# A graph network's edge loop with a ring of 16 gathered groups, node units in three steps, and a prologue in five parts

## The reference

```python
h = jnp.maximum(_layernorm(x, axis=-1), 0.0)
...
h = x @ enc_w + enc_b
h_list = [h]
for l in range(n_layers):
    e = edge_attr @ edge_w[l] + edge_b[l]
    msg = jax.nn.relu(h_list[l][src] + e)
    agg = jax.ops.segment_sum(msg, dst, num_segments=n_nodes)
    z = (1.0 + eps[l]) * h_list[l] + agg
    z = jax.nn.relu(z @ mlp_w1[l] + mlp_b1[l]) @ mlp_w2[l] + mlp_b2[l]
    h_list.append(jax.nn.relu(z))
hcat = jnp.concatenate(h_list, axis=1)
return hcat @ out_w + out_b        # and x is added
```

## Time and profile before

| | us |
|---|---|
| median of 3 timed runs | 6492.11 (6486.08 to 6496.12) |
| span of the profiled execution | 8994.4 |
| first gather starts, in the profiled execution | 111.24 |
| last gather starts, in the profiled execution | 8945.59 |
| POOL busy | 4756.1 |
| PE busy | 5354.3 |
| DVE busy | 1804.5 |
| ACT busy | 1006.8 |

### The profile page before, as it was taken

The page is one execution under the profiler, slowest core; times in us unless marked ns, Lnnn a source line. Parts: engine busy times, 40 slices in busy tenths (PEclk is TensorE's granted clock), DMA queues, the critical chain, the costliest instruction groups (busy, mean ns, idle before and its releaser), DMA issues.

```text
span 8994.4 us, 89832 instructions
## 1 busy us (share of the span) xinstructions
PE 5354.3 (60%) x21970; PEld 4659.5 (52%) x21971; DVE 1804.5 (20%) x4266; ACT 1006.8 (11%) x1630; POOL 4756.1 (53%) x5030
## 2 busy tenths in 40 slices
PE   5565656556565566555665556565556555655556
PEld 4555555555555455555555555554555555555555
DVE  5111111111111111111111111111111111111112
ACT  3111111111111111111111111111111111111111
POOL 4555555555555455555555555545555555555554
PEclk7555555555555555555555555555555555555555
DMA  4111111111111111111111111111111111111112
GB/s 134 44 44 45 44 44 45 44 44 44 43 43 44 41 46 45 45 45 44 44 44 43 45 44 44 45 41 45 44 43 46 44 45 43 44 43 45 44 44 66
DMA packets 342770, 422.04 MB, mean 47 GB/s; under 512 B 183228, under 2 KB 249840, under 8 KB 342624
## 3 DMA queue, kind: packets, MB, share of 16 engines
q0 software_dynamic: 159456, 326.88, 14.2%
q1 hardware_dynamic: 144327, 75.77, 3.3%
q10 hardware_dynamic: 38976, 19.27, 0.7%
HBM read 388.55 MB, written 41.09 MB: 48 GB/s over the span
## 4 chain that ended last, share of the span: by engine, by line
PE 36%; another core or an unknown queue 35%; issue 16%; DVE 5%; DVEq 5%; ACT 2%; ACTq 0%; DMA 0%; POOL 0%; POOLq 0%; SPq 0%
PE bank L562 17%; PE bank L555 14%; DVEq L767 2%; PE bank L587 2%; DVE rows L829 2%; PE bank L593 2%; ACT msg L483 2%; DVE onehot L762 1%; DVEq L230 1%; DVEq L229 1%; DVE agg_t L771 1%; DVEq L771 0%; DVE out_acc L688 0%; PE bank L514 0%
## 5 line engine op out<-in xcount | busy, mean ns | idle before, releaser
L356 POOL DMA_INDIRECT rows<-h_table,idx x4983 | 4713.5, 946 | 4136.4 <-DMA idx<-src_l 1755.2
L562 PE MATMUL bank<-onehot,msg 128*128 128x64 f32 x9984 | 2386.1, 423 | 3046.3 <-ACT msg L483 2080.4
L562 PEld LDWEIGHTS bank<-onehot,msg 128*128 128x128 f32 x9984 | 2191.6, 325 | 3305.6 <-DVE onehot L762 2031.5
L555 PE MATMUL bank<-edgew,attr 17*128 x9984 | 2447.4, 423 | 107.9 <-issue 107.9
L555 PEld LDWEIGHTS bank<-edgew,attr 17*128 17x128 f32 x9984 | 2131.3, 313 | 243.3 <-issue 129.3
L483 ACT ACTIVATE msg<-rows 128x512 f32<-128x512 f32 x1248 | 785.4, 629 | 7085.0 <-DVE rows L829 6582.7
L829 DVE TENSOR_TENSOR rows<-bank,rows 128x512 f32<-128x512 f32 x1248 | 859.9, 689 | 2968.5 <-remote 2069.5
L771 DVE TENSOR_TENSOR agg_t<-bank,agg_t 128x64 f32 x1248 | 280.7, 225 | 3278.1 <-remote 1724.1
L762 DVE TENSOR_TENSOR onehot<-iota,dst_rel 128x256 f32<-128x256 f32 x1248 | 529.4, 424 | 255.3 <-issue 255.3
L587 PE MATMUL bank<-agg_t,w1s 128*128 x336 | 269.5, 936 | 387.8 <-issue 204.8
L587 PEld LDWEIGHTS bank<-agg_t,w1s 128*128 128x128 f32 x336 | 88.1, 301 | 534.7 <-issue 429.4
(11 more groups left out here) (61 smaller groups left out, 324.0 us busy)
## 6 DMA issues: line engine op xcount, KB each, us to landing
rows<-h_table,idx POOLq DMA_INDIRECT x4983
attr<-ea_t SPq DMA_DIRECT2D x624, 64.0 KB
h_table<-h_n ACTq DMA_DIRECT2D x42, 256.0 KB, 2.4
idx<-src_l SPq DMA_DIRECT2D x624, 4.0 KB
h_table<-h_n ACTq DMA_DIRECT2D x42, 192.0 KB, 2.4
out_acc<-x_t SPq DMA_DIRECT2D x7, 896.0 KB, 10.1
h_table<-x_t SPq DMA_DIRECT2D x14, 448.0 KB, 4.1
h_table<-h_n SPq DMA_DIRECT2D x14, 256.0 KB, 2.3
```

Source lines behind the costliest of these rows:

```text
L356: return g.indirect_dma_start(dst, None, h_table, bass.IndirectOffsetOnAxis(ap=index, axis=0))
L555: last = nc.tensor.matmul(dst[:, j * D:(j + 1) * D], cols[:, j * P:(j + 1) * P], edgew[:, bass.ds(l, 1), :].rearrange("p a n -> p (a n)"), ...
L562: last = nc.tensor.matmul(dst[:, 0:WIN], m[:, j, :], hot_m[:, j, :], start=(j == 0), stop=(j == TG - 1))
```

## The change

Seven things change; the edges, the groups of four tiles, the windows of 64 and the arithmetic in float32 stay.

- **Ring.** `rows` holds 16 groups (`RING`) in place of 8. POOL waits for each group rather than each chunk, and for `agg_done` of the group 16 back, since relu now works in place in `rows` and PE reads the messages there. `msg` is gone. SP loads source numbers for 8 groups at once (four buffers) and attributes for 8 groups at once (two buffers).
- **Edge terms.** `attr` holds a group's four tiles in 64 partitions and a row of ones; `edgew` is block-diagonal (65 x 512), and one matmul makes a group's edge terms.
- **Lags.** Three banks for edge terms, three for window sums, four one-hot matrices. PE makes edge terms two groups ahead, and DVE adds window sums two groups behind.
- **Node units** are 4 tiles (`UT`; 25 in a layer, with `NT` = 100), and at most one belongs to each half-body of 8 groups (`unit_at`). PE does its three steps (`node_z`, `node_h`, `node_out`) behind groups 1, 3 and 5, ACT its steps behind groups 3, 5 and 7, and DVE its step behind group 6. One unit is left for the layer's end.
- **Two tables** `h_table[0]` and `h_table[1]`, so source numbers need no offset; `src_l` and the transfers that filled the second half are gone. ACT loads `w1s` and `w2s` at a layer's start. POOL's and ACT's loop over layers is written out.
- **Prologue.** The statistics come in five parts of 20 tiles; a unit of 4 tiles is normalised by ACT (two) and POOL (two); ACT writes both `h_t` and `agg_t` from PSUM, so the copy of line 683 is gone; the 25 units are written out without a loop.
- **Table of units.** DVE works out `unit_at` with some 30 small operations in the prologue, while the third-last unit is under way, and POOL waits for them (`s_ready`) before its first gather; before, POOL did not.

The edge loop's part of the diff:

```diff
+                def edge_bodies(c, spare):
+                    for r in range(4):
+                        wait_apart(g, idx_in[r], c * 16 + (l * (NB // 4) + 1) * 16)
+                        for k in range(HB):
+                            slot = r % 2 * HB + k
+                            wait_apart(g, agg_done, c * (4 * HB) + (l * NG + r * HB + k + S0 - RING + 1))
                             for j in range(TG):
-                                t = k * TG + j
-                                if q * TC + t < TC * CB - spare:
-                                    gather(rows[:, q, t, :], idx[q][:, t:t + 1]).then_inc(gathered[q][k], 16)
+                                if (r * HB + k) * TG + j < 4 * HB * TG - spare:
+                                    gather(l, rows[:, slot, j, :], idx[r][:, k * TG + j:k * TG + j + 1])\
+                                        .then_inc(gathered[slot], 16)
...
-                        for k in range(GC):
...
-                        nc.scalar.activation(msg[k % 2][:, :, :], rows[:, q, t:t + TG, :], ACT.Relu)\
-                          .then_inc(msg_ready, 1)
+                            nc.scalar.activation(rows[:, k, :, :], rows[:, k, :, :], ACT.Relu).then_inc(relued, 1)
+                            if kk in (3, 5, 7):
+                                with act.If(unit > 0):
+                                    (relu_z if kk == 3 else relu_h if kk == 5 else store)(unit_before(unit))
...
             def edge_terms(dst, cols, l):
+                return nc.tensor.matmul(dst[:, :], cols, edgew[:, bass.ds(l, 1), :].rearrange("p a n -> p (a n)"),
+                                        start=True, stop=True)
...
+                        sp.wait_ge(summed, m * HB + (S0 - 3 * HB))
+                        sp.dma_start(idx[r][:, :], src_t[:, bass.ds(b * (HB * TG), HB * TG)])\
+                          .then_inc(idx_in[r], 16)
+                        sp.wait_ge(e_done, m * HB + (S0 - HB))
```

The prologue's copy, the fill of the table and the weights:

```diff
+                nc.scalar.activation(p_ht[i % 2], enc_ps[i % 2][:, :], ACT.Identity, bias=encb[:, 0:1])\
+                  .then_inc(p_h, 1)
+                nc.scalar.activation(agg_t[:, i * UC:(i + 1) * UC], enc_ps[i % 2][:, :], ACT.Identity,
+                                     bias=encb[:, 0:1]).then_inc(p_kept, 1)
...
-                sp.dma_start(h_rows[:, bass.ds(i * TB + NT, TB), :],
-                             x_t[:, bass.ds(i * (TB * D), TB * D)].rearrange("p (t d) -> p t d", d=D))\
-                  .then_inc(s_fill, 16)
...
-                for u in range(2):
-                    sp.wait_ge(h_ready[u], l * NI + (NI + 1))
-                sp.dma_start(w1s[:, :], w1[bass.ds(l, 1), :, :].rearrange("a k n -> (a k) n")).then_inc(s_w, 16)
...
+            def load_weights(l):
+                act.dma_start(w1s[:, :], w1[l, :, :]).then_inc(s_w, 16)
```

More of the change, by code:

```diff
@@ L33 @@
 TG = 4
[L34 to L40, removed]
+HB = 8
+RING = 16
+UT = 4
+UC = UT * P
+XP = 20
+NE_PS = 3
+NA_PS = 3
+NHOT = 4
+S0 = 32
+N0 = 4
 def gnn_kernel(nc, x_t, src_t, dst_t, dst_g, ea_t, enc_w, enc_b, edge_w, edge_b, w1, b1, w2, b2,
@@ new lines, in normalise @@
+            def normalise(i):
+                if i % (XP // UT) == 0:
+                    act.wait_ge(s_norm, i // (XP // UT) + 1)
+                if i >= 2:
+                    act.wait_ge(p_turn, i - 1)
+                for j in range(2):
+                    t = i * UT + j
+                    last = nc.scalar.activation(p_hn[i % 2][:, j, :], out_acc[:, t, :], ACT.Relu,
+                                                bias=nmr[:, t:t + 1], scale=rstd[:, t:t + 1])
+                last.then_inc(p_norm_a, 1)
@@ L452, in _ @@
+            for i in range(NI):
+                if i + 1 < NI:
+                    if (i + 1) % (XP // UT) == XP // UT - 1 and i + 1 < NI - 1:
+                        roots((i + 1) // (XP // UT) + 1)
+                    normalise(i + 1)
+                if i >= 1:
+                    take_h0(i - 1)
             take_h0(NI - 1)
-            with act.Fori(0, NI) as i:
-                seed0(i)
+            for i in range(NI):
+                act.wait_ge(o0_done, i + 1)
+                cols = agg_t[:, i * UC:(i + 1) * UC]
+                nc.scalar.activation(cols, cols, ACT.Identity, scale=eps1[:, 0:1]).then_inc(seeded0, 1)
@@ L558, in edge_terms @@
-                return last
-            def window_sums(dst, m, hot_m):
-                for j in range(TG):
-                    last = nc.tensor.matmul(dst[:, 0:WIN], m[:, j, :], hot_m[:, j, :],
+                    last = nc.tensor.matmul(dst[:, 0:WIN], rows[:, slot, j, :], onehot[:, hot_slot, j, :],
                                             start=(j == 0), stop=(j == TG - 1))
@@ new lines, in node_out @@
+                def node_out(i):
+                    n = l * NI + i
+                    pe.wait_ge(h_ready, n + (1 + N0))
+                    for j in range(UT):
+                        last = nc.tensor.transpose(zt_ps[:, j * P:(j + 1) * P], h_t[:, j * P:(j + 1) * P], ident[:, :])
+                    last.then_inc(tr_done, 1)
+                    for j in range(UT):
+                        last = nc.tensor.matmul(zh_ps[:, j * D:(j + 1) * D], h_t[:, j * P:(j + 1) * P],
+                                                outw[:, bass.ds(l + 1, 1), :].rearrange("p a n -> p (a n)"),
+                                                start=True, stop=True)
+                    last.then_inc(o_done, 1)
```

921 lines of the change are left out of this document (472 added, 449 removed).

## The result

The changed kernel takes 6540.8 us (median of 4 runs, 6536.7 to 6544.5) where the kernel before takes 6493.4: a ratio of 1.0075, 95% interval 1.0061 to 1.0089. It is 47 us slower. The forecast was 6483, with a range to 6560 that holds the time, but with the sign the other way. That the range holds it is luck: its upper end was the price of instruction fetches, of which the runs show none.

The account below looks back on a forecast made before the run. POOL was taken to bound the kernel: 4983 gathers at 1.25 us, 6229 us, 96% of the timed median. 6492 - 1 (prologue) - 5 (layer changes) - 3 (end) = 6483 us, -0.14%; range 6405 to 6560.

Parts of the forecast that it names:

- the sign: Whole kernel: slightly faster, 6483 us against 6492, -0.14%.
- The gathers' cadence: POOL's gathers: still 4983, one every 1.25 us, 6229 us in all; change 0 us, upper bound 94 us.
- The 85 us above the sum: Timed median of before over the 6407 us built from pieces; time around the span, gather jitter or short waits, undecided.
- rival 1: The 85 us are POOL's waits, which the ring of 16 takes away: 6407 us, half of them 6445; chance 0.22.
- the 15 us around a kernel: Barriers and resets around a kernel, on the order of 15 us, would be a part of the 85.
- The standstill: Other engines nearly stand still in long gather bursts: 2470 us of POOL's waits, in the profiled execution, next to none timed.
- The rest of the sum: Prologue -1, layer changes -5 in all and end -3 us, taken from 6492 to give 6483.
- Layer changes: From a layer's last gather to the next layer's first: -2.5 us each (-5 to 0), -5 in all.
- End: After the last gather: a smaller last unit and a store of 4 tiles, -3 us (-6 to 0).
- Prologue: Ahead of the first gather: earlier start -19, units +9, table +9, sum -1 us; bounds -6 and +8, or +21.
- Ring, edge terms and node units inside the body: Edge loop: 0 us each, as POOL finds no wait to lose and PE's work lies beside the gathers.
- Rivals 2 and 3: Cadence 1.25 us is the profiler's, some 5300 us (chance 0.06); GpSimd's longer loop waits for fetches, 53 to 101 us (0.10).

Follow-up runs that it names:

- b_nohot: The kernel before without one-hots in its edge loop (two are made ahead of it; output partly wrong): 6415.1 us, 0.990 of before.
- b_lag2: The kernel before with DVE adding window sums two groups behind in place of one; a register instruction came with it: 6459.9 us, 0.998 of before.
- a_nohot: The changed kernel without one-hots in its edge loop (four are made ahead of it; output partly wrong): 6410.2 us, 0.989 of before.
- a_psum: The changed kernel with one input of the one-hot in PSUM in place of SBUF, and two banks for window sums: 6413.1 us, 0.989 of before.

## Why the prediction was wrong, step by step

*The gathers' cadence.* This is the step that failed: "Still 4983, of 128 rows of 512 B each. 0 us." The 1.25 us came from bursts of before in which DVE nearly stood still by the very standstill that I had set aside, so hardly a gather there could be held by it: in that trace 68 of the 1248 one-hots begin 0.02 to 0.22 us ahead of a gather's start. I took a number that needs DVE idle into a kernel in which DVE works beside every gather, and asked only whether POOL waits longer between gathers, not whether a gather itself takes longer. Measured: 66 us on top in before (b_nohot), about 131 in the changed kernel (6541 less 6410, on two chips). The clue stood in the trace: it had 59 long gathers, 58 of them under a one-hot. The prediction gives them no price. That one-hots hold gathers, and by how much at each place, is shown; why more of them fall on a start in the changed kernel is open in part (b_lag2).

*The 85 us above the sum*, of which rival 1 made waits for a free place in the ring. They were mostly held gathers: without one-hots before takes 6415.1 us, 8 above the sum, and POOL has no wait in it. Nor do they hold the 15 us around a kernel that the prediction takes from the Trainium skill ("Runtime: NRT & Kernel Launch", "The launch sequence"): a run's time stands 1.8 us above its span here. The rival fails, and the doubt it stood for was well placed: here sat the term that decided the sign.

*The standstill.* I put it down to the profiled execution. That the timed runs of before had none was right, the cause was not. Where it comes back, timed runs have it, and the changed kernel was 14.5% faster there.

*The rest of the sum.* Layer changes: -1.5 and -2.4 us (forecast -2.5 each). End: 20.2 against 22.7, -2.5 (forecast -3). Prologue: 118.1 against 110.4 in b_nohot, +8, the upper bound that I gave, where I took -1. So these parts add up to +1, not to -9. The times without one-hots, 6410.2 and 6415.1 us, differ by -5, which is within what such runs differ by (6395.5 to 6412.5 for a_nohot). Three terms of the prologue were mis-sized. The start: normalising begins at 17.1 us in place of 28.4, 11 earlier and not 19. The units up to the table: 79 us against 74 for before's 14 iterations, +5, where I put 75 against 66, +9. What lies behind them: from the table's start at 95.93 to the first gather at 118.07 are 22.1 us, where before had 8.1 (102.3 to 110.4), +14 in place of +9. The units themselves are fast, 2.1 us of POOL each (two tiles 0.89, the add 1.27) where I had put 3, but POOL waits at each new part of 20 tiles, since DVE works out that part's scale only behind the last unit of the one before:

```profile
68.61 0.89 POOL L316 TENSOR_SCALAR rows<-out_acc,rstd,nmr 128x128 f32<-128x128 f32 x2 [6.12 <-DVE nmr L665]
...
85.48 0.89 POOL L316 TENSOR_SCALAR rows<-out_acc,rstd,nmr 128x128 f32<-128x128 f32 x2 [6.33 <-DVE nmr L665]
```

Five units take 85.48 - 68.61 = 16.9 us, 3.4 each, of which 6.3 are this wait, four times in the prologue. Ring, edge terms and node units inside the body: 0 us, as forecast, since POOL does not wait.

*Rivals 2 and 3.* A gather is 1.25 us without any waits, so the cadence is not the profiler's. Instruction packets rose from 4 and 7 to 6 and 21, no "issue" stands at even distances, and POOL's idle time per gather is 0.32 us as before: GpSimd's longer body costs nothing. This agrees with the rule of the Trainium skill ("Runtime: NRT & Kernel Launch", "Instruction fetch mechanics") that I had weighed.

*The sign.* +65 for the held gathers, -5 for the rest, give +60; measured +47. The difference lies within what before's excess moves from job to job: before less a kernel without held gathers was 66, 76 and 115 us in three of them (the last two against changed kernels' 6400 and 6408, and so only rough), and 78 in the job of the result if 6415 holds there. Why it moves is not shown.

The Trainium skill ("SBUF — State Buffer", "Who interferes with whom") says that a VectorE instruction with two SBUF inputs contends with a GpSimd instruction that reads SBUF, its second input coming through the read interface that they share, and that issue order decides who blocks. The traces agree: with both inputs in SBUF a gather that starts 0.1 us into the one-hot is 0.20 us longer, with one in PSUM it is not. The other order shows too: one-hots that begin in the last 0.03 us ahead of a gather's start take 0.47 us in place of 0.42 (0.42 in a_psum), and that gather is not held. The same section also reports that `tensor_tensor` was not seen to stall a DMA, as generating descriptors needs the write interface, which it calls inferred. For these gathers the measurement says otherwise. I had cited other pages and passed this one by.

## What to carry to other kernels

Where GpSimd issues gathers back to back, look for each VectorE operation with two inputs in SBUF (here a `tensor_scalar` from SBUF to SBUF held gathers too) and ask whether it can begin just ahead of a gather's start; put one input in PSUM, or move it by a wait. A duration that was read while another engine stood still is a lower bound, not the price beside that engine's work. When a sum of floors misses the timed run by more than the effect forecast, that rest is the first thing to find, and a change with "nothing on the path" can still shift phases by 0.1 us and lose 1%. An edit that is meant to move one thing moves others: compare the distances in both traces before it is called a test.

## What the runs showed of the hardware

A gather was held by one-hots that were under way some 0.12 us behind its start, and up to their end: one-hots that begin 0.25 to 0.95 us behind a start cost 0.00 us, those 0.02 to 0.22 ahead of one 0.17 us on average, in 737 of 1248 cases in the changed kernel. That it reads its indices at that moment was not tested.

A gather that follows at once starts 1.25 us behind the one before whatever waits lie between (every four, every eight), so long as they are met.

PE's matmuls come more slowly in the standstills even where they wait for nothing: in before's second profile PE started 4 instructions from 140 to 150 us, 38 from 116 to 120. Each takes 0.37 us there; the rest is idle time ahead of it, which no other engine ends (the granted clock, 0.50 against 1.00, is far from accounting for it). One such row, and the two windows, columns as in the earlier trace rows:

```profile
140.18 0.37 PE L514 MATMUL bank<-outw,agg_t 128*128 128x128 f32 x1 [2.43 <-issue]
```

```profile
116.00:120.00 4.00, 4.00 (x38) 4.00 (x37) 1.82 (x5) 1.30 (x3) 2.94 (x4) 1.00 0.18 49
...
140.00:150.00 10.00, 1.49 (x4) 1.15 (x4) 0.69 (x1) 0.72 (x1) 7.54 (x8) 0.50 0.20 52
```
